# Turning the attention sums to token rows with 36 of the identity's 128 columns

## What is computed

```python
q, k, v = heads(x @ Wq.T + bq), heads(ctx @ Wk.T + bk), heads(ctx @ Wv.T + bv)   # 16 heads of 8
scores = q @ k.T / sqrt(8);  scores = where(mask == 0, -1e9, scores)
context = softmax(scores) @ v              # 16 heads x 56 tokens x 8
x = x + tanh(g) * (rows(context) @ Wo.T + bo)
```

## Time and profile before

| | |
|---|---|
| median of 3 runs | 790.48 us (790.0 to 791.91) |
| the profiled execution's own time | 790.32 us |
| its span in the profile | 788.5 us |
| busy: TensorE matmul, weight load | 679.7 us (86%), 475.0 us (60%) |
| busy: VectorE, ScalarE, GpSimd | 534.8 us, 510.0 us, 270.4 us |
| mean granted clock of TensorE | 0.965 of full |

### The profile page before, as it was taken

The page is one execution under the profiler, slowest core; times in us unless marked ns, Lnnn a source line. Parts: engine busy times, 40 slices in busy tenths (PEclk is TensorE's granted clock), DMA queues, the critical chain, the costliest instruction groups (busy, mean ns, idle before and its releaser), DMA issues.

```text
span 788.5 us, 19444 instructions
## 1 busy us (share of the span) xinstructions
PE 679.7 (86%) x7276; PEld 475.0 (60%) x7283; DVE 534.8 (68%) x1252; ACT 510.0 (65%) x807; POOL 270.4 (34%) x322
## 2 busy tenths in 40 slices
PE   3599899986369889889889889889899999799997
PEld 2477777764226555555555655555566666468777
DVE  5799999998778768678768768768767771311122
ACT  4477777776226777687776777777778768343531
POOL 3388888883233222222231241241242010000000
PEclk9899999999589999999999999999999999799999
DMA  4122222254524736626625724734744670110110
GB/s 137 39 79 79 78 84 94 94 153 29 112 73 89 172 74 127 154 54 127 152 71 111 166 77 92 166 93 84 158 118 94 124 169 15 48 43 28 54 40 24
DMA packets 59377, 74.40 MB, mean 94 GB/s; under 512 B 35320, under 2 KB 40178, under 8 KB 59306
## 3 DMA queue, kind: packets, MB, share of 16 engines
q1 hardware_dynamic: 59306, 73.39, 39.4%
HBM read 32.35 MB, written 1.40 MB: 43 GB/s over the span
## 4 chain that ended last, share of the span: by engine, by line
PE 51%; DVE 10%; issue 7%; ACT 4%; POOL 2%; DVEq 0%; ACTq 0%; POOLq 0%
PE ps L734 10%; PE ps L649 7%; PE ps L807 6%; PE ps L795 6%; DVE mx L1574 6%; PE ps L641 6%; PE ps L721 5%; PE ps L635 4%; PE ps L669 2%; ACT P L985 1%; ACT KP L928 1%; POOL Qb L1109 1%; DVE silu L1480 1%; ACT Vp L911 1%; ACT silu L943 1%
## 5 line engine op out<-in xcount | busy, mean ns | idle before, releaser
L985 ACT ACTIVATE P<-ps,kbias,kscale 125x896 f32<-125x896 f32 x192 | 210.5, 1098 | 91.5 <-PE ps L721 88.8
L1574 DVE TENSOR_REDUCE mx<-ps 128x1 f32<-128x500 f32 x336 | 215.5, 673 | 78.4 <-PE ps L649 74.6
L649 PE MATMUL ps<-KP,Qb 128*128 128x500 bf16 x336 | 129.0, 386 | 5.4 <-DVE mx L1574 4.3
L734 PE MATMUL ps<-P,Vp 125*32 125x112 f32 x3072 | 113.8, 266 | 1.6 <-ACT P L985 1.1
L734 PEld LDWEIGHTS ps<-P,Vp 125*32 125x32 f32 x3072 | 67.4, 109 | 51.6 <-issue 30.0
L1095 POOL TENSOR_TENSOR KP<-kvall,KP 128x1500 bf16<-128x1500 f32 x16 | 48.5, 3032 | 141.1 <-ACT KP L928 141.1
L526 PE MATMUL ps<-wkv,cT 128*125 128x256 f32 x384 | 91.8, 383 | 1.0 <-ACT arena L885 1.0
L526 PEld LDWEIGHTS ps<-wkv,cT 128*125 128x125 f32 x384 | 69.3, 190 | 9.9 <-issue 1.3
L885 ACT ACTIVATE arena<-ps,arena 125x128 f32<-125x128 f32 x192 | 54.8, 368 | 27.9 <-DVE arena L1279 13.9
L721 PE MATMUL ps<-QS,KS 128*128 128x112 bf16 x768 | 69.8, 214 | 3.3 <-issue 1.9
L721 PE MATMUL ps<-QS,arena 128*128 128x112 bf16 x768 | 67.5, 213 | 5.0 <-issue 5.0
(11 more groups left out here) (212 smaller groups left out, 1010.2 us busy)
## 6 DMA issues: line engine op xcount, KB each, us to landing
cT<-ctxT_dram SPq DMA_DIRECT2D x32, 750.0 KB, 4.2
KS<-KP SPq DMA_DIRECT2D x48, 375.0 KB, 7.2
arena<-KP SPq DMA_DIRECT2D x48, 375.0 KB, 7.4
QS<-QD SPq DMA_DIRECT2D x96, 28.0 KB, 5.6
wgu<-w_dram SPq DMA_DIRECT2D x8, 256.0 KB, 3.1
silu<-w_dram SPq DMA_DIRECT2D x8, 256.0 KB, 2.8
x<-xh_dram SPq DMA_DIRECT2D x1, 512.0 KB, 3.6
mixed<-att SPq DMA_DIRECT2D x16, 28.0 KB
```

Source lines behind the costliest of these rows:

```text
L649: ins = nc.tensor.matmul(ps[:, bank, 0:KCW], q[:, 128 * c:128 * c + 128], KP[par][0][:, KCW * k:KCW * k + KCW], start=True, stop=True)
L734: ins = nc.tensor.matmul(ps[r:r + PW, 7, c:c + PAIRW], Vp[par][0:TK, t, p, :], P[t % 2][0:TK, PAIRW * p:PAIRW * p + PAIRW], start=(t == 0 ...
L985: nc.scalar.activation(P[t % 2][0:TK, :].rearrange("p (k n) -> p k n", k=2), src, ACT.Exp, scale=kscale[0:TK, bass.ds(n, 1)], bias=kbias[0 ...
L1574: ins = v.tensor_reduce(mx[:, c, k:k + 1], ps[:, bank, 0:KCW], AX.X, ALU.max)
```

## The change

Each of OT's four matmuls streams 36 columns of the identity in place of 128: from each group of 32 columns (one pair) nine, that is columns 0 to 8 for the first head (denominator, then numerators) and 9 to 17 for the second (numerators, then the denominator). For the second head the denominator must stand behind its numerators, so `Vp` gets a second column of ones, column 17, set by GpSimd beside the first. The outputs lie 64 columns apart in the bank (`OTW`), shifted by 8 for the first head so that every denominator is at 8 + 9q; `heads` reads them there. Shapes on VectorE are as before (16 denominators, twice 64 products). No instruction moves to another place; the changed file has one line more ahead of the named ones.

```diff
--- before.py
+++ after.py
@@ -29,6 +29,7 @@
 KCW = S2 // KC
 PAIRW = 2 * S
 PW = 32
+OTW = 64
 NPAIR = H // 2
 SLOTS = 2 * NG
 KVW = D + H
@@ -663,11 +664,13 @@
                                                        start=True, stop=True)
                 elif unit == "OT":
                     pe.wait_ge(sem("o_ready"), b + 1)
+                    wanted = ident[:].rearrange("p (q n) -> p q n", q=4)
                     for c in range(2):
                         for k in range(2):
-                            lhs = O[:, PAIRW * c + S * k:PAIRW * c + S * k + S]
-                            ins = nc.tensor.matmul(ps[HALF * par:HALF * par + S, bank, 128 * (2 * c + k):128 * (2 * c + k) + 128],
-                                                   lhs, ident[:], start=True, stop=True)
+                            lhs, at0 = O[:, PAIRW * c + S * k:PAIRW * c + S * k + S], OTW * (2 * c + k) + DK * (1 - k)
+                            lo = (DK + 1) * k
+                            ins = nc.tensor.matmul(ps[HALF * par:HALF * par + S, bank, at0:at0 + 4 * (DK + 1)],
+                                                   lhs, wanted[:, :, lo:lo + DK + 1], start=True, stop=True)
                 elif unit == "FT":
                     pe.wait_ge(sem("an_ready"), 2 * b + 2)
                     ins = nc.tensor.transpose(ps[:, bank, 0:D], an[:], ident[:])
@@ -1064,7 +1067,8 @@
             ins.then_inc(sem("zeroed"), 1)
             pool.wait_ge(sem("zeroed"), 1)
             for n in range(2):
-                ins = nc.gpsimd.memset(Vp[n][:, :, :, 0:1], 1.0)
+                nc.gpsimd.memset(Vp[n][:, :, :, 0:1], 1.0)
+                ins = nc.gpsimd.memset(Vp[n][:, :, :, 1 + 2 * DK:2 + 2 * DK], 1.0)
             ins.then_inc(sem("filled"), 1)
 
 
@@ -1585,8 +1589,8 @@
 
                 bank, r = bank_of(at, "OT"), slice(HALF * par, HALF * par + S)
                 dve.wait_ge(sem("aux_ready"), filled(at, "OT"))
-                src = ps[r, bank, :].rearrange("p (c k q n) -> p k c q n", c=2, k=2, q=4)
-                v.reciprocal(rden[r, :, :], ps[r, bank, :].rearrange("p (g q n) -> p g q n", g=4, q=4)[:, :, :, 0]
+                four = ps[r, bank, 0:4 * OTW].rearrange("p (g n) -> p g n", g=4)
+                v.reciprocal(rden[r, :, :], four[:, :, DK:DK + 4 * (DK + 1)].rearrange("p g (q n) -> p g q n", q=4)[:, :, :, 0]
                              ).then_inc(sem("rden_ready"), 1)
                 dve.wait_ge(sem("rden_ready"), b + 1)
                 if par == 0 and "FT" in units(at):
@@ -1594,8 +1598,9 @@
                 dst = an[r, :].rearrange("p (c q k d) -> p k c q d", c=2, q=4, k=2)
                 rd = rden[r, :, :].rearrange("p (c k) q -> p k c q", c=2)
                 for k in range(2):
-                    ins = v.tensor_tensor(dst[:, k], src[:, k, :, :, 1 + DK * k:1 + DK * k + DK],
-                                          bc(rd[:, k], 3, [S, 2, 4, DK]), ALU.mult)
+                    lo = (DK + 1) * (1 - k)
+                    src = four[:, k::2, lo:lo + 4 * (DK + 1)].rearrange("p c (q n) -> p c q n", q=4)[:, :, :, 0:DK]
+                    ins = v.tensor_tensor(dst[:, k], src, bc(rd[:, k], 3, [S, 2, 4, DK]), ALU.mult)
                 ins.then_inc(sem(free_of(at, "OT")), 1)
                 dve.wait_ge(sem(free_of(at, "OT")), emptied(at, "OT"))
                 v.memset(spare[:], 0.0).then_inc(sem("an_ready"), 1)
```

## The result

The changed kernel took 783.68 us (median of 5, 782.69 to 785.39), the kernel before beside it 791.91 us (5, 790.0 to 792.07): so 8.2 us less by the medians. The ratio over all executions is 0.9906, with a 95% interval of 0.9887 to 0.9925, which stands for 7.4 us. In a second set on another occasion it was 786.06 against 792.29 us, 6.2 us less by the medians, with a ratio of 0.9915 (0.9895 to 0.9934), which stands for 6.7 us. The profiled execution took 783.08 us with a span of 781.2 us, 7.3 us less than the span before.

What follows compares the result with a forecast made beforehand. TensorE was taken to bound the kernel, with all OT matmul time on the path. 16 turnings shortened by 0.52 us gave 8.3 us: 790.32 - 8.3 = 782.0, forecast 782.2 us, range 779.6 to 786.8.

Steps and rivals of the forecast that it cites:

- What bounds, and that all 16 turnings are path: TensorE bounds; each turning (eight OT matmuls, 1.01 to 1.08 us) lies on the chain of waits, 16 in all.
- The load takes over at 0.052 us a record: OT's records, stream-bound at 0.115 us, become bound by loading 56 columns, 0.052 us each.
- The turning 0.52 us shorter: Each OT turning goes from 1.08 to 0.56 us; times 16 that is 8.3 us.
- the last record: The last matmul of each OT turning streams 92 columns fewer, saving 0.077 us.
- In series: Rival, 16%: OT's load and stream don't overlap, 0.087 us a record, 4.4 us gained, 786.1 us.
- issue pace: Rival, 10%: OT's loads hide deeper, 0.0325 us a record as in the weighing, 10.5 us gained, 780.0 us.
- Nothing for the short runs, VectorE's strides and the ones: Four-run reads in OT, VectorE's changed strides and GpSimd's two extra memsets were each costed at nothing.
- What is late next: Behind OT no wait takes the gain back; VectorE's 0.59 us wait is used up almost exactly.
- ScalarE's wait of 1.59 us: ScalarE's gap in the window stage (at 417.99) was to stay as it is.
- The clock: Rival, 4%, slower: TensorE's clock falls in the windows, 1.8 us a fall; one in every window makes 811 us.
- Busy time: TensorE's matmul busy time at OT's line was to fall by more than 8 us.
- The sum: Whole kernel: profiled 790.32 us less 8.3 is 782.0; forecast 782.2 us, as the profile lay 0.16 under the median.

Runs made afterwards that it cites:

- e5_twice: Changed kernel with every matmul of OT issued twice, 16 records in place of 8; 793.88 us in one execution (kernel before 793.31).
- e9_split: Changed kernel with each of OT's matmuls split by tokens into 32 and 24; 784.34 us in one execution (kernel before 793.31).
- e2_one_run: Changed kernel with the 36 streamed columns in one contiguous run in place of four runs of nine; 786.74 us (kernel before 793.31).
- e7_only_ones: Kernel before with the second column of ones alone; 792.88 us against 792.29, ratio 0.9999.
- e3_half_load: Changed kernel loading 28 of 56 columns of O, stream still 36 columns; 778.69 us in one execution (kernel before 792.43).
- e10_split_side: Changed kernel with OT in the side bank and its matmuls split into 32 and 24 tokens; 775.52 us, ratio 0.9787 to the kernel before.
- e8_64_columns: Changed kernel streaming 16 columns of each pair in place of 9, 64 in all; 787.30 us in one execution (kernel before 792.43).
- e6_side_bank_5: Changed kernel with OT in the side bank in place of the two banks of the maxima; 780.41 us, ratio 0.9839 to the kernel before.

## Why the prediction was right, point by point

- *What bounds, and that all 16 turnings are path.* Right. The chain has all 16, at 0.53 to 0.60 us; in e5_twice a pair of windows grew by what was added to its two turnings.
- *The load takes over at 0.052 us a record.* Right: 0.054 as a mean, 0.051 or 0.052 from the third record on. But one of its two rows was read wrongly. The weighing's 0.0325 us is not the price of a load of 32 columns, nor a limit for the issue of records: e9_split has pairs of loads of 32 and 24 in 0.034. The weighing's records stream 112 columns each (the row at 412.00), 0.093 us at the stream's rate, and in the trace they start in fours, 0.007 us apart within a four and 0.096 from one four to the next once they are under way, which fits four streams beside each other. So the line had one sound point, the router's 0.112 us for 128 columns. By proportion that gives 0.049 for 56; that the other point led to 0.052 is in part luck.
- *The turning 0.52 us shorter.* Measured 0.48. Seven distances gave 7 x 0.061 = 0.43 (forecast 0.44). The term that was mis-sized is the last record: 92 columns fewer were to save 0.077 us, but its length went only from 0.273 to 0.219, 0.054. 16 x 0.48 = 7.7 us in place of 8.3. So it is partly luck that the medians of the first set lie 8.2 us apart: its ratio stands for 7.4, the spans of the profiled executions differ by 7.3, and the second set's ratio stands for 6.7.
- *The rivals.* "In series" (0.087 us a record) and "issue pace" (0.0325) both fall to the measured 0.054, and the short runs to e2_one_run.
- *Nothing for the short runs, VectorE's strides and the ones.* Right (e2_one_run at the same 0.60; reciprocal and products still 0.26 and 0.37; e7_only_ones at 0.9999).
- *What is late next.* Right: no new wait. That the slack was thin is right too: e3_half_load and e9_split ran into the wait at MX6. Wrong is that ScalarE's wait of 1.59 us would stay: it became 1.11, since TensorE's scores come 0.48 us sooner behind ScalarE's work before them.
- *The clock.* Half missed. The earlier trace rows show a mean of 1.00 for 400 us, and I took the stage as free of falls; one of 3 to 4 us was in it. The rival's price of a fall, 1.8 us, was too high (1.2 to 1.6 measured), and the five additional falls that would have used up the gain did not come. But falls are a part of what blurs the second set.
- *Busy time.* I expected over 8 us less of TensorE's; line 672 has 7.7 less, and the whole only 4.3. Up to the first OT TensorE was busy 207.5 us in place of 206.4, from there to the last OT 359.9 in place of 365.5, and behind it 108.0 in place of 107.8. So 1.2 us came back outside the windows and some 1.6 within them; 7 records more in the trace are a part of that, and the rest is not shown.
- *The sum.* In the profiled executions: the first OT 0.06 us earlier; from it to the last OT 401.33 us became 393.93, 7.40 less (15 turnings are 7.2, and the one fall there cost less than the one before); behind the last OT's start 116.75 became 116.91, although that turning gave 0.48. There the router's matmuls took 3.58 us as before, and the experts' first ones had more of their time at the lower clock (mean granted clock 0.84 against 0.89):

```profile
670.38 3.58 PE L785 MATMUL ps<-gw_sb,xT 128*128 128x8 f32 x16 [0.45 <-ACT xT L1006]
673.81 14.55 PE L798 MATMUL ps<-xT,wgu 128*128 128x448 f32 x32
```

14.55 us for 32 of them, where the kernel before had

```profile
681.88 13.76 PE L795 MATMUL ps<-xT,wgu 128*128 128x448 f32 x32
```

With -0.06 - 7.40 + 0.16 = -7.3 us the difference of the spans is divided by place; not every part of the 0.16 has its cause shown. The forecast 782.2 us against 783.68 lies low by 1.5, most of it because the same kernel before read 790.48 then and 791.91 beside the changed one.

## What to carry to other kernels

In a stream of small f32 matmuls, compare the two prices of a record, columns streamed and columns loaded, from rows of the same trace. Here they overlapped and the longer one counted, so cutting the longer one paid only down to the other. Take the rows from records that run one behind the other: a pace of records that run in fours is the price of neither. If the stationary operand is between 32 and 64 columns wide, try to split it into two groups of at most 32: in this kernel (56 as 32 and 24) the same work then ran side by side, and the idle stretch against its 32-column neighbours went. Expect the next wait: at 28 columns, and with both changes of e10_split_side, TensorE began to wait for VectorE. And when a turning on the critical path is shortened, look at which bank it shares and what follows it: the two waits at its ends together were worth nearly as much (0.44 us) as its columns (0.48).

## What the runs showed of the hardware that I had not expected

- 32- and 24-column loads with 36-column streams in two column groups go at 0.017 us a record, against 0.032 for 28-column loads in one group (e3_half_load) and 0.054 for 56 columns.
- The length of a record, as the trace gives it, is 0.273 us for 128 columns, 0.219 for 64 and for 36, and 0.204 for 18: it does not follow the stream from 64 to 36 columns.
- The weighing's records (32 columns loaded, 112 streamed) start four at a time, 0.007 us apart, every 0.096 us.
- TensorE's clock fell to 1.2 GHz for 3 to 4 us inside a stage where TensorE is nine tenths busy, behind stretches of 2.7 to 2.8 us with 0.8 to 1.2 us of work, in up to three of the six such gaps (e8_64_columns), and in none of them in e6_side_bank_5 and e10_split_side. A mean clock of 1.00 over a long stretch hides it.
